# A fused attention and feed-forward layer in fp32: the second batch projected by whole weights, probabilities regrouped pair by pair, new engine orders

## What is computed

```python
xn = _layernorm(x)                                  # 8 x 256 x 128
x2 = (xn - mean) / sqrt(var + 1e-5) * ln_w + ln_b   # heads' input
q, k, v = (einsum('bsd,hde->bshe', x2, W) + b for W, b in ...)   # 16 heads of 64
scores = where(causal, einsum('bqhe,bkhe->bhqk', q, k) / 8, -inf)
z = einsum('bhqk,bkhe->bqhe', softmax(scores), v)
attn = einsum('bqhe,hed->bqd', z, W_o) + b_o
ffn = relu(xn @ Wq1.T + b1) @ Wq2.T + b2            # 128 -> 512 -> 128, ternary weights
out = x + attn + ffn
```

## Time and profile before

| what | value |
|---|---|
| median of three runs | 224.38 us |
| the profiled execution | 225.33 us |
| its span, first to last instruction | 223.5 us |
| granted TensorE clock | 1.00 of full speed throughout |
| busy PE, DVE, ACT, POOL | 95%, 90%, 87%, 83% of the span |
| data moved | 30.79 MB, mean 138 GB/s |
| regrouping transfers (L351) | 124, of 192 KB each |

### The profile page before, as it was taken

One profiled execution on the slowest core, in us unless ns is written; L12 is line 12 of the kernel. 1 busy time (PEld: TensorE's weight loads), 2 busy tenths in 40 slices (PEclk: granted clock), 3 DMA queues, 4 the chain that ended last, 5 costly groups with the idle time before them and its releaser, 6 DMA issues.

```text
span 223.5 us, 9672 instructions
## 1 busy us (share of the span) xinstructions
PE 211.9 (95%) x3670; PEld 187.9 (84%) x3670; DVE 201.8 (90%) x776; ACT 195.5 (87%) x733; POOL 184.8 (83%) x363
## 2 busy tenths in 40 slices
PE   7999799999999999999998999989999999999795
PEld 5766498888998899889987999879998998899584
DVE  3499999999999999999999999999999999999931
ACT  0999999997999899997999899997999899996830
POOL 5799989999988989798988899797988985996530
PEclk9999999999999999999999999999999999999999
DMA  5990656606675487636855566636756567677700
GB/s 155 279 273 6 141 116 172 143 3 144 146 158 127 105 196 174 133 78 153 172 134 150 123 147 159 121 84 143 173 119 177 109 152 171 153 165 161 165 5 23
DMA packets 24030, 30.79 MB, mean 138 GB/s; under 512 B 2608, under 2 KB 23088, under 8 KB 23984
## 3 DMA queue, kind: packets, MB, share of 16 engines
q1 hardware_dynamic: 23840, 30.16, 57.5%
q10 hardware_dynamic: 144, 0.02, 0.0%
HBM read 4.73 MB, written 1.05 MB: 26 GB/s over the span
## 4 chain that ended last, share of the span: by engine, by line
PE 46%; ACT 16%; DVE 14%; POOL 11%; DMA 7%; SPq 3%; issue 2%; POOLq 0%; DVEq 0%
PE s_ps L822 8%; DMA pT<-blocks 7%; PE m_ps L862 7%; ACT prob L491 5%; DVE s_ps L603 4%; ACT prob L493 4%; PE m_ps L940 4%; DVE blocks L616 3%; SPq L351 3%; PE m_ps L787 3%; POOL prob L315 3%; ACT qk L480 2%; PE m_ps L789 2%; PE m_ps L788 2%; ACT qk L482 2%; POOL prob L314 2%
## 5 line engine op out<-in xcount | busy, mean ns | idle before, releaser
L491 ACT ACTIVATE prob<-s_ps,neg_max 128x256 f32<-128x256 f32 x128 | 67.6, 528 | 5.6 <-DVE neg_max L603 5.2
L315 POOL TENSOR_SCALAR prob<-prob,inv_sum 128x256 f32<-128x256 f32 x126 | 61.3, 486 | 0.0
L616 DVE STREAM_TRANSPOSE blocks<-prob 128x768 f32<-128x768 f32 x62 | 59.7, 968 | 1.6 <-POOL prob L315 1.6
L314 POOL TENSOR_SCALAR prob<-prob,inv_sum 128x128 f32<-128x128 f32 x126 | 47.5, 377 | 15.4 <-DVE inv_sum L610 15.4
L603 DVE CUSTOM_DVE_ANT_0 s_ps<-s_ps,causal 128x256 f32<-128x256 f32 x128 | 55.1, 430 | 5.0 <-PE s_ps L822 4.5
L493 ACT ACTIVATE prob<-s_ps,neg_max 128x128 f32<-128x128 f32 x128 | 54.0, 422 | 0.0
L862 PE MATMUL m_ps<-pT,v 64*64 64x64 f32 (+2 forms) x1536 | 49.0, 256 | 3.5 <-DMA pT<-blocks 2.1
L822 PE MATMUL s_ps<-qk 64*64 64x128 f32 (+2 forms) x1280 | 49.9, 276 | 0.9 <-ACT prob L493 0.5
L862 PEld LDWEIGHTS m_ps<-pT,v 64*64 64x64 f32 x1536 | 42.5, 133 | 8.8 <-DVE zT_lo L622 3.6
L822 PEld LDWEIGHTS s_ps<-qk 64*64 64x64 f32 x1280 | 42.0, 133 | 7.1 <-issue 3.8
L603 DVE CUSTOM_DVE_ANT_0 s_ps<-s_ps,causal_first 128x128 f32<-128x128 f32 x128 | 42.4, 331 | 0.0
(11 more groups left out here) (120 smaller groups left out, 492.4 us busy)
## 6 DMA issues: line engine op xcount, KB each, us to landing
pT<-blocks SPq DMA_DIRECT2D x124, 192.0 KB, 3.6
xT_cur<-in_xT SPq DMA_DIRECT2D x8, 128.0 KB, 4.2
outT<-out_sb SPq DMA_DIRECT2D x8, 128.0 KB, 4.0
x_all<-in_x SPq DMA_DIRECT2D x1, 768.0 KB, 8.6
wv_raw<-in_w_v SPq DMA_DIRECT2D x2, 256.0 KB, 5.5
wo<-in_w_o SPq DMA_DIRECT2D x1, 512.0 KB, 6.5
x_all<-in_x SPq DMA_DIRECT2D x2, 128.0 KB, 3.9
wq_raw<-in_w_q SPq DMA_DIRECT2D x2, 128.0 KB, 2.5
```

Of the source, the lines that this page charges most:

```text
L314: op(first, first, inv_sum[:, j, 2 + h:3 + h], 0.0, ALU.mult, ALU.add)
L315: last = op(later, later, inv_sum[:, j, h:h + 1], 0.0, ALU.mult, ALU.add)
L491: nc.scalar.activation(later, s_ps[:, pair % 2, h, 0:S].rearrange("p (g j k) -> p g j k", g=TILES, j=QT), ACT.Exp, bias=neg_max[:, j, h:h ...
L616: nc.vector.transpose(blocks[:, duo, :, n, :, :], prob[:, pair % NBUF, :, :, :, :] .rearrange("p h j g k -> p (j g) h k")).then_inc(turned, 1)
```

## The change

1. A constant WHOLE = 2: batches 0 and 1 are projected by whole fp32 weights and input (before, batch 0 alone). Batch 1 no longer waits for parted weights, and its x2T is neither split on ACT (`xh+` is gone from ACT_HEAD) nor on POOL (`xl+` is gone from POOL_HEAD). Parted weights are needed from batch 2 on. The 12 weight splits stay, and most come later in the orders.
2. `blocks` and `pT` are laid out by pair instead of by duo. SP regroups pair by pair (d0 to d7), with four transfers each that move half the bytes: 248 transfers of 96 KB instead of 124 of 192 KB, each with 128 pieces, of 768 bytes instead of 1,536. The wait for a free `pT` is unchanged in kind, and the heads' products wait for both pairs of a duo.
3. All orders are written anew, and the borders between HEAD, PLAN and TAIL shift: PE's HEAD now holds pr2, pr3 and s0 of batch 2.

```diff
+WHOLE = 2
-PE_PLAN = ("pr2:0 pr3:3 x0-:2 s0 y0-:1 s1 z0- pr4:3 pr5:0 x1-:1 y1-:2 s2 z1- pr6:3 v0:0 x2-:2 y2-:1 s3 z2- s4 "
-           "v1:0 pr7:3 x3-:2 y3-:1 s5 z3- s6 v2:3 v3:0 xh+:2 oa-:1 f0:2 f1:3 s7 pr0+:2 pr1+:0 xn+:3 ob-")
+PE_PLAN = ("x0-:1 y0-:2 s1 z0- pr4:0 pr5:3 x1-:1 y1-:2 s2 z1- pr6:0 v0:3 x2-:1 y2-:2 s3 z2- s4 v1:0 pr7:3 x3-:1 "
+           "y3-:2 s5 z3- s6 v2:0 v3:3 xh+:1 oa-:2 f0:0 f1:1 s7 pr0+:0 pr1+:3 xn+:1 ob- pr2+:0 pr3+:3 s0+")
-DVE_PLAN = ("i7- m0 m1 ln+ m2 z0- t7- m3 i0 m4 m5 z1- i1 t0 v0 m6 i2 m7 z2- m8 m9 v1 t1 i3 m10 m11 z3- v2 t2 m12 "
-            "xh+ t3 i4 m13 i5 v3 m14 m15 t4 i6 t5 xn+ o- t6")
+DVE_PLAN = ("z0- m2 i0 m3 t7- m4 z1- m5 v0 ln+ m6 m7 z2- i1 m8 m9 t0 v1 m10 i2 m11 i3 z3- m12 v2 t1 m13 xh+ t2 i4 "
+            "v3 i5 t3 m14 i6 m15 t4 t5 xn+ o- t6 m0+ i7 m1+")
-PE_HEAD  = "xb:2 pr0:3 pr1:0 xn:2 s0 pr2:1 ... v3:3 f1:1 xh+:2 xn+:0 s6 pr0+:3 s7 pr1+:2 x0:1 pr2+:3 y0:0 s0+ z0 bo:2 ..."
+PE_HEAD  = "xb:1 pr0:0 pr1:1 xn:2 s0 v0:3 ... v3:1 xh+:0 s5 f1:2 xn+:3 pr0+:0 pr1+:1 s6 s7 x0:2 y0:3 pr2+:0 z0 s0+ bo:1 ..."
-ACT_HEAD = "wh0 wh1 pr0 wh2 pr1 wh3 xn ... f1 e12 pr0+ e13 wh4 pr1+ e14 e15 z0 wh5 e0+ ..."
+ACT_HEAD = "wh0 wh1 pr0 pr1 wh2 xn ... f1 pr0+ e12 e13 pr1+ z0 e14 e15 e0+ ... z2 wh3 e5+ ... wh4 ... wh5 ..."
-POOL_HEAD = ("hs np wl2 wl3 ln+ p0 p1 p2 p3 h0 xl+ p4 p5 p6 h1 p7 wl4 wl5 p0+ ln++ p1+ ol p2+ p3+ p4+ xl++ p5+ p6+")
+POOL_HEAD = ("hs np p0 ln+ p1 p2 wl2 h0 p3 p4 p5 p6 h1 p7 ln++ p0+ wl3 p1+ ol p2+ p3+ xl++ p4+ p5+ wl4 p6+ h0+ p7+ "
+             "p0++ wl5")
-SP_PLAN = ("d2 d3 st- d0+ d1+")
+SP_PLAN = ("d2 d3 d4 d5 d6 d7 d0+ st- d1+")
...
-        blocks = sb("blocks", [P, DUOS, QT * 3, 2, 2, QB])
-        pT = sb("pT", [P, DUOS, QT, 3, 2, 2, QB])
+        blocks = sb("blocks", [P, PAIRS, QT * 3, 2, QB])
+        pT = sb("pT", [P, PAIRS, QT, 3, 2, QB])
...
-            def regroup(b, duo):
-                wait(sp, turned, PAIRS * b + 2 * duo + 2)
-                wait(sp, z_psd, 4 * (DUOS * (b - 1) + duo + 1))
+            def regroup(b, pair):
+                wait(sp, turned, PAIRS * b + pair + 1)
+                wait(sp, z_psd, 4 * (DUOS * (b - 1) + pair // 2 + 1))
                 for i in range(QT):
                     rows = slice(i * QB, i * QB + QB)
-                    sp.dma_start(pT[:, duo, i, :, :, :, :].rearrange("p g n h q -> p (g n h q)"),
+                    sp.dma_start(pT[:, pair, i, :, :, :].rearrange("p g h q -> p (g h q)"),
...
             def heads_input(b):
-                wait(dve, xh_hi, b)
+                if b < WHOLE:
+                    wait(dve, xh_psd, b)
+                else:
+                    wait(dve, xh_hi, b - WHOLE + 1)
...
-                    if b == 0:
-                        wait_weights_of_pair(n, pair)
+                    if b < WHOLE:
+                        if b == 0:
+                            wait_weights_of_pair(n, pair)
                         last = nc.tensor.matmul(dst, raw[kind][:, cols], x2T[:, :], start=True, stop=True)
                         continue
-                    if b == 1 and pair % (PAIRS // 2) == 0:
+                    if b == WHOLE and pair % (PAIRS // 2) == 0:
...
-                        pe.wait_ge(pT_in[duo], 16 * QT * (b + 1))
+                        for pair in (2 * duo, 2 * duo + 1):
+                            pe.wait_ge(pT_in[pair], 16 * QT * (b + 1))
```

More of the change, by code:

```diff
@@ L48 @@
 BUSY = (5, 1)
-PE_HEAD = ("xb:2 pr0:3 pr1:0 xn:2 s0 pr2:1 pr3:0 s1 v0:3 s2 v1:2 ta:3 pr4:0 pr5:1 s3 pr6:3 v2:2 s4 pr7:3 f0:0 s5 "
[3 rows of a table removed]
-PE_PLAN = ("pr2:0 pr3:3 x0-:2 s0 y0-:1 s1 z0- pr4:3 pr5:0 x1-:1 y1-:2 s2 z1- pr6:3 v0:0 x2-:2 y2-:1 s3 z2- s4 "
-           "v1:0 pr7:3 x3-:2 y3-:1 s5 z3- s6 v2:3 v3:0 xh+:2 oa-:1 f0:2 f1:3 s7 pr0+:2 pr1+:0 xn+:3 ob-")
-PE_TAIL = ("pr2:0 pr3:2 s0 x0-:0 x1-:3 s1 y0-:1 pr4:2 z0- s2 y1-:2 z1- x2-:0 y2-:1 s3 z2- pr5:3 v0:2 s4 pr6:3 "
-           "v1:1 pr7:0 x3-:3 y3-:2 s5 x0:1 z3- s6 oa-:0 ob- y0:2 s7 z0 v2:0 v3:3 x1:1 f0:2 y1:0 z1 tw6:3 f1:2 "
-           "tw7:3 x2:0 tn3:2 y2:1 x3:2 z2 y3:3 z3 oa:1 ob oc")
@@ L58 @@
[L58 to L64, removed]
@@ L65 @@
-DVE_HEAD = ("lz nh xb wl0 m0 m1 xn ln+ m2 m3 v0 m4 m5 wl1 th i0 v1 i1 te0 m6 m7 i2 t0 t1 m8 i3 m9 m10 v2 t2 m11 "
[3 rows of a table removed]
-DVE_PLAN = ("i7- m0 m1 ln+ m2 z0- t7- m3 i0 m4 m5 z1- i1 t0 v0 m6 i2 m7 z2- m8 m9 v1 t1 i3 m10 m11 z3- v2 t2 m12 "
-            "xh+ t3 i4 m13 i5 v3 m14 m15 t4 i6 t5 xn+ o- t6")
-DVE_TAIL = ("m0 i7- m1 m2 m3 i0 t7- z0- m4 t0 z1- i1 m5 m6 z2- m7 t1 i2 m8 v0 m9 i3 v1 t2 m10 i4 t3 m11 z3- m12 "
-            "i5 m13 t4 o- t5 i6 m14 m15 z0 v2 i7 v3 q7 z1 n3 z2 z3 o")
-POOL_HEAD = ("hs np wl2 wl3 ln+ p0 p1 p2 p3 h0 xl+ p4 p5 p6 h1 p7 wl4 wl5 p0+ ln++ p1+ ol p2+ p3+ p4+ xl++ p5+ p6+")
@@ L74 @@
-POOL_PLAN = ("h0- p7- h1- p0 p1 ln+ p2 p3 xl+ p4 p5 p6")
-POOL_TAIL = ("p7- p0 h0- p1 h1- p2 p3 p4 p5 p6 h0 h1")
-SP_HEAD = ("d0 d1 d2 d3 d0+ d1+ d2+ d3+ d0++ st d1++")
-SP_PLAN = ("d2 d3 st- d0+ d1+")
-SP_TAIL = ("d2 st- st")
+PE_HEAD = ("xb:1 pr0:0 pr1:1 xn:2 s0 v0:3 pr2:0 pr3:1 s1 s2 pr4:0 ta:3 v1:2 pr5:3 s3 pr6:2 v2:1 pr7:0 s4 f0:3 "
[3 rows of a table added]
+PE_PLAN = ("x0-:1 y0-:2 s1 z0- pr4:0 pr5:3 x1-:1 y1-:2 s2 z1- pr6:0 v0:3 x2-:1 y2-:2 s3 z2- s4 v1:0 pr7:3 x3-:1 "
+           "y3-:2 s5 z3- s6 v2:0 v3:3 xh+:1 oa-:2 f0:0 f1:1 s7 pr0+:0 pr1+:3 xn+:1 ob- pr2+:0 pr3+:3 s0+")
@@ new lines @@
+PE_TAIL = ("s1 x0-:1 y0-:0 pr4:2 z0- s2 x1-:3 y1-:2 z1- x2-:1 y2-:0 s3 z2- v0:2 pr5:3 s4 pr6:1 v1:3 pr7:0 x3-:1 "
+           "y3-:2 s5 z3- s6 oa-:3 x0:2 ob- y0:1 s7 z0 v2:0 v3:3 f0:2 x1:1 y1:0 f1:3 tw6:2 z1 tw7:2 tn3:3 x2:1 "
+           "y2:0 x3:2 z2 y3:3 z3 oa:1 ob oc")
+ACT_HEAD = ("wh0 wh1 pr0 pr1 wh2 xn e0 e1 pr2 aa pr3 e2 e3 e4 e5 pr4 pr5 e6 pr6 pr7 e7 f0 e8 e9 xn+ e10 e11 f1 "
+            "pr0+ e12 e13 pr1+ z0 e14 e15 e0+ pr2+ e1+ pr3+ pr4+ e2+ z1 e3+ pr5+ e4+ pr6+ z2 wh3 e5+ e6+ e7+ oh "
+            "z3 e8+ pr7+ wh4 e9+ xh++ e10+ e11+ wh5 f0+ f1+ e12+ xn++ e13+ e14+ pr0++ pr1++ e15+ pr2++")
@@ new lines @@
+ACT_PLAN = ("pr3 e0 z0- e1 pr4 e2 pr5 z1- e3 e4 e5 pr6 z2- e6 e7 e8 e9 pr7 z3- e10 xh+ e11 e12 f0 f1 e13 pr0+ e14 "
+            "pr1+ xn+ e15 pr2+")
+ACT_TAIL = ("pr3 e0 e1 pr4 z0- e2 e3 z1- e4 z2- e5 e6 pr5 e7 pr6 e8 e9 z3- e10 e11 pr7 e12 e13 z0 e14 e15 f0 f1 "
+            "w6 z1 w7 z2 z3")
+DVE_HEAD = ("lz nh xb m0 m1 xn v0 ln+ i0 wl0 m2 m3 m4 th m5 v1 t0 m6 i1 te0 i2 m7 v2 t1 m8 m9 xh+ m10 v3 m11 i3 "
[3 rows of a table added]
+DVE_PLAN = ("z0- m2 i0 m3 t7- m4 z1- m5 v0 ln+ m6 m7 z2- i1 m8 m9 t0 v1 m10 i2 m11 i3 z3- m12 v2 t1 m13 xh+ t2 i4 "
+            "v3 i5 t3 m14 i6 m15 t4 t5 xn+ o- t6 m0+ i7 m1+")
@@ new lines @@
+DVE_TAIL = ("m2 m3 t7- i0 z0- m4 m5 i1 z1- m6 m7 z2- t0 v0 i2 m8 t1 m9 i3 t2 v1 m10 m11 i4 t3 z3- m12 i5 m13 t4 "
+            "o- i6 t5 m14 m15 z0 v2 v3 i7 q7 z1 n3 z2 z3 o")
+POOL_HEAD = ("hs np p0 ln+ p1 p2 wl2 h0 p3 p4 p5 p6 h1 p7 ln++ p0+ wl3 p1+ ol p2+ p3+ xl++ p4+ p5+ wl4 p6+ h0+ p7+ "
+             "p0++ wl5")
+POOL_PLAN = ("h1- ln+ p1 p2 p3 xl+ p4 p5 p6 p7 h0 p0+")
+POOL_TAIL = ("p1 h1- p2 p3 p4 p5 p6 h0 h1")
+SP_HEAD = ("d0 d1 d2 d3 d4 d5 d6 d7 d0+ d1+ d2+ d3+ d4+ d5+ d6+ d7+ d0++ d1++ st")
@@ L81, in steps @@
+SP_PLAN = ("d2 d3 d4 d5 d6 d7 d0+ st- d1+")
+SP_TAIL = ("d2 d3 d4 d5 st- st")
 def steps(plan, batch):
@@ L203, in attention_ffn_kernel @@
         vec_in = sem("vec_in")
-        pT_in = [sem(f"pT_in{n}") for n in range(DUOS)]
+        pT_in = [sem(f"pT_in{n}") for n in range(PAIRS)]
         out_done = [sem(f"out_done{n}") for n in range(2)]
@@ L316, in divide_by_sums @@
             return last
-        pT_last = pT[:, DUOS - 1, :, :, :, :, :].rearrange("p i g n h q -> p (i g n h q)").rearrange("p (n h w) -> p n h w", n=2, h=2)
+        pT_last = pT[:, PAIRS - 2:PAIRS, :, :, :, :].rearrange("p n i g h q -> p n (i g h q)").rearrange("p n (h w) -> p n h w", h=2)
         block = ctx.enter_context(nc.Block())
@@ L344, in _ @@
             load_turned(1)
-            def regroup(b, duo):
-                wait(sp, turned, PAIRS * b + 2 * duo + 2)
-                wait(sp, z_psd, 4 * (DUOS * (b - 1) + duo + 1))
+            def regroup(b, pair):
+                wait(sp, turned, PAIRS * b + pair + 1)
+                wait(sp, z_psd, 4 * (DUOS * (b - 1) + pair // 2 + 1))
                 for i in range(QT):
                     rows = slice(i * QB, i * QB + QB)
-                    sp.dma_start(pT[:, duo, i, :, :, :, :].rearrange("p g n h q -> p (g n h q)"),
-                                 blocks[rows, duo, :, :, :, :].rearrange("k c n h q -> k (c n h q)")
-                                 .rearrange("k (j r) -> k j r", j=QT)).then_inc(pT_in[duo], 16)
+                    sp.dma_start(pT[:, pair, i, :, :, :].rearrange("p g h q -> p (g h q)"),
+                                 blocks[rows, pair, :, :, :].rearrange("k c h q -> k (c h q)")
+                                 .rearrange("k (j r) -> k j r", j=QT)).then_inc(pT_in[pair], 16)
             def store(b):
@@ L613, in turn_blocks @@
                 wait(dve, prob_ready, PAIRS * b + pair + 1)
```

(24 more changed lines are left out.)

## The result

The changed kernel takes 252.56 us (median of four runs, 251.33 to 255.35) against 224.39 us: 1.124 of the time before, with an interval of 1.118 to 1.130. The longest of the four, 255.35 us at a granted clock of 0.960 where the others had 0.973 to 0.980, is not in that ratio. The kernel is 28 us slower, and outside the range that was given (220.2 to 228.0). The second rival named the mechanism, SP's queue, at a chance of 0.25, and put it at 228 us.

What follows compares the result with a forecast made beforehand. PE's own work was taken as the bound, DVE close behind. Profiled 225.33 + 0.6 (head) - 0.9 (regrouping waits) - 1.3 (steady order) = 223.7 us, or 222.8 against the median of 224.38; range 220.2 to 228.

Steps and rivals of the forecast that it cites:

- second rival: From d1 to d7, SP's queue becomes the bound because halving bytes helps nothing: 227 to 232 us, say 228; chance 0.25.
- SP's queue: Regrouping by pair on SP: 2.5 us a pair, PE's waits for pT fall from 2.1 to 1.2 us, so -0.9.
- What bounds the kernel: Whole kernel: PE's work sets the pace, some 24.4 us of a 25.11 us steady batch, with DVE not far behind.
- sign of being wrong: At SP's regrouping: four issues taking 2.6 us or more while PE's waits for pT grow would refute the forecast.
- the formula: SP's lateness when t7 is done: six pairs' issues less DVE's 12.5 us; at 2.5 us a pair, 2.5 us late.
- The count for d5: Pair 5's regrouping lands at t7 + 2.0 us, against PE wanting it at t7 + 2.7: not late.
- Whole products: Batch 1's projections: PE gets 2.0 us more work with 0.36 us to spare, so +2.0 us.
- The head's wait of 1.4 us: Before batch 1's first projection, PE's wait for the copy of the last values goes with the new order: -1.4 us.
- fourth rival: ACT and POOL paced the head, so it gives -1.4 in place of +0.6: 220.8 us against the median; chance 0.18.
- The steady order: Steady batches: DVE reaches z steps sooner, so weight loads wait less for z's low part: -1.3 us, between 0 and 3.4 gained.
- The rule of the Trainium skill: Regrouping transfers: batch them; 2.0 us fixed plus bytes over 436 GB/s, so a halved one lands only about 0.2 us sooner.
- third rival: Regrouping: halves land no sooner and DMA waits stay, 0 in place of -0.9: 224.4 us against the median; chance 0.17.

Runs made afterwards that it cites:

- e15: New orders and whole second batch, duos 0 and 1 regrouped by duo, pairs 4 to 7 by pair, against the kernel before: 242.04 us, ratio 1.077.
- e14: The changed kernel with three of a pair's four transfers in every batch, a quarter of the regrouping left out: 223.15 us, 0.993 of the kernel before.
- e1: The changed kernel with regrouping by duo again, four 192 KB transfers each; new orders and whole products stay: 231.15 us, 1.027 of the kernel before.
- e2: The kernel before with regrouping by pair alone; old orders, only batch 0 projected whole: 230.21 us, ratio 1.025.
- e3: The kernel before with the second batch projected whole, nothing else changed: 224.79 us against 224.86, ratio 0.999.
- e13: The changed kernel with two of a pair's four transfers in every batch, half of the regrouping left out: 222.88 us, 0.990 of the kernel before.
- e8: The changed kernel with two of a pair's four transfers from batch 1 on, batch 0 keeping all four: 227.12 us, 1.010 of the kernel before.

## Why the prediction was wrong

**What bounds the kernel** was read rightly: PE's and DVE's work is as long after as before, and the steady batch grew by waits, in one of four with 0.9 us for a lower clock on top (last section).

**SP's queue: the step that failed**, in three terms: the size of an issue in a burst, the moment at which PE wants the pairs, and what lateness costs. The prediction's own sign of being wrong, four issues of 2.6 us or more and growing waits for pT, came true.

First, the size of an issue. I read the 3.11 us for a duo's four issues as draining, took 2.5 us a pair with half the bytes, and kept 2.3 to 3.1 as the ends. Half of that was right: the rise within a group of four is gone, and a plain group takes four issues of 0.60 and the gaps, 2.5 us. But 19 of the 248 issues take 1.0 to 2.1 us (the rows above show 1.87, and 1.93 in e15), and a burst holds two or three of these: 2.93 us a pair in the batch shown. That is beyond the 2.58 us at which the rival had put the point of decision. DVE's time for the burst was about right, 13.2 us measured and 12.5 counted. With the mean issue of the whole trace, 0.665 us and 0.045 between, a pair is 2.84 us and the formula gives 6 x 2.84 - 13.2 = 3.8 us of lateness, where batches 2 to 5 have 4.0 to 4.6. The formula is nearly right, and the term that failed in it is the issue.

Second, the need. I took PE's wish from the old orders: duo 3 at t7 + 6.8, duo 2 at t7 + 2.7. In the new orders it is t7 + 5.6 and t7 + 1.5 (e14). The count for d5, t7 + 2.0 and so "not late", fails at both ends: in batches 2 to 5 of the changed kernel pair 5 lands 3.2 to 3.6 us after t7, and duo 2 has almost as much of PE's waits as duo 3. In e1, with the old transfers, the earlier need alone makes PE wait for duo 3 in each of batches 2 to 5, 1.2 to 1.7 us. I had also not compared the burst with that of the old orders: there t7 ends 15.5 to 16.5 us after t1. Pairs in the old orders (e2) leave SP 2.0 to 3.2 us late in batches 1 to 6 and cost 5.4 us; with the new orders' 13.2 us it is 3.9 to 5.3 us late, and that costs 28.

Third, the price of lateness. The rival let half of it be absorbed "as DVE slows along" and priced itself at 228. Measured, little is absorbed. The burst stays as tight as it was: t7 ends 13.21 us after t1 in each of batches 2 to 5, whatever the batch's length. In batches 2 to 4 the products of duo 3 start 9.5 us after t7 on average, 3.9 later than in e14 undisturbed; from there to the next t7 it is 18.7 us instead of 19.3, so that 0.6 of the 3.9 is absorbed and 3.3 come back in every batch. From t7 of batch 2 to t7 of batch 5 a batch is 28.2 us in the changed kernel and 24.9 in e14. The stretches up to 57.90, 200.27 and the end are 3.6, 16.5 and 5.9 us longer than their like before (54.33, 180.20, 223.5), 26.0 between the two profiles: every batch pays. The bound by SP's whole load, +1.3 us a batch, was too low too, because SP stands in each batch until the next t0 and t1 are turned (from 133.8 to 136.1 and from 140.1 to 141.3), and that time cannot be used.

**Whole products**: +2.0 us forecast, 0.5 us in the stretch, 0 in the time (e3). The 0.43 and 0.34 us of a product are right, and e3 shows 0.43 again (30.26 to 30.69 to 31.13). What failed is that PE had only 0.36 us to spare: a stretch in which PE counts as 99% busy still took in 1.5 us of work. The busy time is no measure of that room; how it came about was not tested.

**The head's wait of 1.4 us**: its removal could not be seen apart. In e14 the whole head is shorter: PE reaches the end of batch 1's stretch at 52.84 against 54.33 before (nearly the same point: the order of two steps there differs), and the products of batch 1's duo 3 at 70.74 against 71.75. The forecast had +0.6 there; without SP's queue it is -1.0 to -1.5, the fourth rival's value. That ACT and POOL had been the pace is not shown by it.

**The steady order** was to give 1.3 us by fewer waits for the low part of z. e14 has 6.0 us of them in place of 3.6. The reason given was wrong. The steady batch does get shorter, 24.9 us in e14 against 25.1 in the earlier trace rows, but the kernel before has its three waits for pT in these batches (2.1 us), so that a gain from the orders themselves is not shown.

**The sum without the queue** would have been close: 222.8 forecast, 223.15 and 222.88 measured in e14 and e13. With head, order and waits all off in their sizes, that is luck as much as skill.

**The rule of the Trainium skill** on batching (DMA: Bandwidth & Descriptors, section Bandwidth) pointed the right way, and the third rival, which went with it, drew no cost from it. Landing fell from 3.6 to 2.4 us, more than the 0.2 estimated from that page, whose fit is for transfers issued from GpSimd, where these are issued from SP. So the landing was not what cost. What cost was the issue on SP's queue, in the median 0.60 us for 96 KB and 0.62 us for 192 KB.

## What to carry to other kernels

Count a queue's issues as instructions of an engine, at a price each that here hardly depended on the bytes, and compare them with the time between the first and the last event of the burst that releases them, not with the whole period. Take the moment at which the consumer wants each part from the order that will run, not from the old one. Below the knee the count was free here (24 transfers, spread evenly, in e14); beyond it most of the lateness came back in every round of the loop. Take the mean of such an issue, with its rare long ones, and not the median: a burst holds two or three of them. And orders made for one granularity of transfers must be measured with it: the new orders with the whole products are 0.7 to 1% better when a quarter or half of the regrouping is left out, 2.7% worse with duos, 12% worse with pairs.

## What the runs showed of the hardware

The issue of a transfer between SBUF partitions, in 128 pieces, takes SP's queue 0.60 us in the median for 96 KB (mean 0.67, the changed kernel) and 0.62 us for 192 KB (mean 0.75, the kernel before); the load of 768 KB of x, with twelve rows a partition, takes 0.59 us in the kernel before. Long issues of 1.0 to 2.1 us turn up among them in every kernel here; what makes them was not found out.

PE's waits cost a little twice. In the changed kernel PE's clock was granted at less than full in two of the six stretches above (0.94). In the second of these PE was busy for 25.82 us for the same work that takes 24.18 at 1.00, the 2.4 GHz level, in its neighbours, and the stretch is 0.9 us longer than they are. In the stretch up to 57.90 it was 25.82 as well, where e14 has 24.16 for the like stretch at 1.00. Around one wait, from 127 to 133 us, the mean was 0.72, and from 130 to 133 us it was 0.50, the 1.2 GHz level:

```profile
127.00:133.00 6.00, 3.84 (x84) 3.75 (x87) 3.29 (x18) 2.89 (x13) 5.04 (x8) 0.72 0.54 129
```

PE had stood for 2.16 us before its product at 129.28. It happened three times in this execution: PE had stood for 2.06 us before 47.57, and for 2.89 us before 214.40, and from 215 to 218 us the clock was 0.50 again. Not every such wait does it: after 2.74 us before 192.89 the clock stayed at 1.00. So up to some 5 us of PE's work in the 28 went with the clock, an estimate from three times 1.64 us; what of it reached the time is not shown. e8 shows what one such fall costs where little else waits: five of its ten executions had a mean clock of 0.992 and took 227.4 to 228.3 us, the other five had 1.000 and took 225.4 to 226.9. In the profiled execution of the kernel before the clock was 1.00 throughout.
